# Attention on one core: a new order for VectorE's and ScalarE's instructions in the second half of each group of eight slots

## The chip, the cores and the metric

The kernel runs on one core of one Trainium2 chip. Time is that of one execution on the device, in microseconds (us). A core has five engines with queues of their own, each of which works through its instructions in the written order: TensorE (PE in the profile), VectorE (DVE), ScalarE (ACT), GpSimd (POOL) and SyncE (SP, which here issues DMAs). They meet through semaphores alone.

## The reference

Eight batches of 512 tokens with 256 features go through attention with 16 heads of 64, and then through a feed-forward network with ternary weights. In short:

```python
xn = layernorm(x)                                   # 8 x 512 x 256
q, k, v = heads(xn @ w_q), heads(xn @ w_k), heads(xn @ w_v)
sim  = (l2norm(q) * exp(scale)) @ l2norm(k).T       # per head, 512 x 512
attn = softmax(sim)
x = x + layernorm((attn @ v) @ w_out + b_out)
h = silu(lin(ln(x), w1)) * lin(ln(x), w2)
h = gelu(lin(gelu(lin(h, h1)), h2))
out = x + layernorm(lin(h, w3))
```

All of it is float32. The kernel multiplies in a rounded float32 type and keeps the accuracy by splitting an operand into a high part (the rounded value) and a low part (what the rounding left), so that most products are two or three matmuls.

## The kernel before, in words

The attention runs in 256 *slots* (`NU`), two to a head, and the program text of every engine is a loop over them. Eight slots are one *quad*, the work of four heads; `r = i % 8` is the place in the quad, and `i32_ = i % 32` the place in a batch. In slot i TensorE computes the scores of slot i (`scores`, L1047 and L1048), multiplies the probabilities of slot i - 2 with the values (`values`, L1064), and does its share of the projections for the next quad: the q and k tiles (`qk_tile`) where `tiles_of` names one, the value tiles (`v_tiles`), the turning of q and k of a pair of heads (`turn`, L1033, at r = 0 and r = 5: first k, then q), and at r = 7 the output projection of the quad before (`outp`, L1078). At i32_ = 19 and 20 it turns the next batch's normalised input (`x_turn`, L998) for the next quad's tiles.

ScalarE takes the scores out of PSUM through the exponential (`exp`, L504, writes `P`), rounds them (`p_high`, L509, writes `Ph`), evacuates a finished head every second slot (`evacuate`, L515), squares a q and k tile (`square`, L483), and writes the high parts of the turned operands (`turn_high`, L496) and of the input (`x_high`, L468). VectorE writes the low parts: of the probabilities (`p_low`, L717, writes `Pl`; slot i treats i - 1), of the turned operands (`turn_low`, L711, writes `turned`) and of the input (`x_low`, L671, writes `xl`). It also sums the squares (`head_sums`, L687), scales the tile when GpSimd has the roots (`head_scale`, L696), divides a pair of heads by their softmax sums (`normal`, L733, reads what a DMA has spread from the table `rows`), and writes the low part of that (`o_low`, L739, writes `nl`), when GpSimd has copied the high part (`o_high`, L381, writes `nh`). At i32_ = 12 and 13 GpSimd also normalises the next input and adds the last batch's result to its input (L395).

What orders this across the engines is a set of waits on counted semaphores. Those that matter here:

- `values(u)` waits for `pl` of u: TensorE at r = 7 needs the low part of the probabilities of r = 5.
- `exp(i)` waits for `pl` of i - 2.
- `outp` of a quad waits for `nl` of both its pairs. The later pair's `normal` is at r = 5 and its `o_low` at r = 6 in the loop of VectorE; both instances of `outp` stand at r = 7 in that of TensorE.
- `o_high` on GpSimd waits for `normal`, and `o_low` for `o_high`.
- The DMAs that stack the turned operands for `scores` (SP, L258 and L259) wait for all four parts of the pair; the pair turned at r = 5 is first used at the next r = 0.
- Three PSUM banks (`M.G`, called bank0 to bank2) are shared by everything but scores and values. A table computed ahead (`PLAN`) gives each user a bank and names the user before it, and `wait_bank` makes TensorE wait until that one's high and low parts are both out.

For the seven quads at whose r = 5 `i32_` is 21, the table gives the turned q of that slot the bank of the next input's first half: `PLAN["Tq", 6]` is `(0, ("x", 2))`, and so on in steps of 8 to `("Tq", 54)` behind `("x", 14)`. So TensorE's second turning at i32_ = 21 waits until `x_high(b + 1, 0)` and `x_low(b + 1, 0)` are done. The second half's bank is next used by `outp`.

Of the kernel before, what the change touches and what calls it, by code (L numbers as in the profile page):

```python
# [5 lines left out]
B, S, D, H, DH = 8, 512, 256, 16, 64  # L6
# [9 lines left out]
NP = B * HP  # L16
# [41 lines left out]
def slot(i):  # L58

    g, c = divmod(i, 2)  # L60
    return g, c, g // H, i % 8, i < NU


def tiles_of(i):

    todo = {6: [(i // 8 + 2, 0)], 0: [(i // 8 + 1, 1)], 1: [(i // 8 + 1, 2)], 2: [(i // 8 + 1, 3)]}.get(i % 8, [])
    return [NT * Q + t for Q, t in todo if Q < NQ]
# [8 lines left out]
def pair_of(i):  # L76

    n = 2 * (i // 8) + {0: 1, 5: 2}.get(i % 8, NP)
    return n if n < NP else None
# [376 lines left out]
def act_program(q, M):  # L456
# [7 lines left out]
    def x_high(b, k):  # L464
        bank = PLAN["x", 2 * b + k][0]
        q.wait_ge("xT", 2 * b + k + 1)
        q.wait_ge("v", 16 * b)
        e.activation(M.xh[:, k, :], M.G[bank][:, :], ACT.Copy).then_inc(S["xh"])  # L468
# [29 lines left out]
    def exp(i):  # L498
        q.wait_ge("s", i + 1)
        q.wait_ge("sh", 2)  # L500
        q.wait_ge("pl", i - 1)
        q.wait_ge("wl", WPOS[1])
        h = (i // 2) % H
        e.activation(M.P[:, i % 2, :], M.SB[i % 2][:, :], ACT.Exp, bias=M.sh[:, h:h + 1]).then_inc(S["exp"])  # L504
# [6 lines left out]
    def evacuate(g):  # L511
        q.wait_ge("pv", 2 * g + 2)
        q.wait_ge("on", 2 * (g // 2 - 1))
        q.wait_ge("wl", WPOS[6])
        e.activation(M.Ev[:, g % 4, :], M.OB[:, :], ACT.Copy).then_inc(S["ev"])  # L515
# [58 lines left out]
    split_w(7)  # L574
    for i in range(SLOTS):
        g, c, b, r, live = slot(i)
        if b + 1 < B and i % 32 == 21:
            x_high(b + 1, 0)
            x_high(b + 1, 1)
        if live:  # L580
            exp(i)
            p_high(i)
        if i % 2 and 0 <= i // 2 - 1 < NG:
            evacuate(i // 2 - 1)
        if i < 3:
            split_w(4 + i)
        if i in (5, 6, 12, 13):
            split_wo(i - 5 if i < 7 else i - 10)
        for u in tiles_of(i):
            square(u)  # L590
        if values_of(i) is not None:
            v_high(values_of(i))
        if pair_of(i) is not None:
            turn_high(pair_of(i), 1)
            turn_high(pair_of(i), 0)
        if HEAD <= i < HEAD + 7:
            for m in MS[i - HEAD]:
                gate(0, 0, m)
                high0(0, m)
        if copy_at(i) is not None:  # L600
            copy_piece(copy_at(i))
        if i in LOADS:
            load_piece(LOADS.index(i))
        if i == NU - 3:
            x3_high(0)
# [28 lines left out]
def vector_program(q, M):  # L634
# [32 lines left out]
    def x_low(b, k):  # L667
        bank = PLAN["x", 2 * b + k][0]
        q.wait_ge("xh", 2 * b + k + 1)
        q.wait_ge("v", 16 * b)  # L670
        e.tensor_tensor(M.xl[:, k, :], M.G[bank][:, :], M.xh[:, k, :].bitcast(f32), ALU.subtract).then_inc(S["xl"])  # L671
# [12 lines left out]
    def head_sums(u):  # L684
        q.wait_ge("sq", u + 1)
        q.wait_ge("rs", u - 1)
        e.reduce_sum(M.ss[:, u % 2, :], M.sq[:, :].rearrange("p (h d) -> p h d", d=DH), AX.X).then_inc(S["ssum"])  # L687
# [18 lines left out]
    def turn_low(n, j):  # L706
        bank = PLAN["Tk" if j else "Tq", n][0]
        q.wait_ge("thk" if j else "thq", n + 1)
        wait_stacked(q, n - 1)
        high, low = (1, 0) if j else (2, 3)  # L710
        e.tensor_tensor(M.turned[:, low, :], M.G[bank][:, :], M.turned[:, high, :].bitcast(f32), ALU.subtract  # L711
                        ).then_inc(S["tlk" if j else "tlq"])
# [14 lines left out]
    def normal(n):  # L727
        q.wait_ge("nl", n - 1)
        for odd in range(2):
            own = slice(64 * odd, 64 * odd + 64)  # L730
            q.wait_ge(f"rb{n % 2}{odd}", 16 * (n // 2 + 1))
            q.wait_ge("ev", 2 * n + odd + 1)
            e.tensor_tensor(M.on[own, n % 2, :], M.Ev[own, (2 * n + odd) % 4, :], M.Rb[own, n % 2, :],  # L733
                            ALU.mult).then_inc(S["on"])
# [147 lines left out]
    for i in range(SLOTS):  # L882
        g, c, b, r, live = slot(i)
        i32_, pb, tail, n = i % 32, i // 32 - 1, i - NU, i // 4 + 1
        early = i % 4 == 1 and i32_ != 21
        if b + 1 < B and i32_ == 21:
            x_low(b + 1, 0)
        if 0 <= i - 1 < NU:
            p_low(i - 1)
        if i < 3:  # L890
            split_w(4 + i)
        if i in (5, 6, 12, 13):
            split_wo(i - 5 if i < 7 else i - 10)
        if i % 4 == 2 and 0 <= n - 3 < NP:
            o_low(n - 3)
        if early and 0 <= n - 3 < NP:
            normal(n - 3)
        if 0 <= pb < B - 1:
            for t in {8: (0, 1), 10: (2,), 11: (3,)}.get(i32_, ()):
                finish(pb, t)  # L900
            if i32_ == 12:
                for t in range(NT):
                    out_scale(pb, t)
        if b + 1 < B:
            for t in {3: (0,), 4: (1, 2, 3)}.get(i32_, ()):
                ln1(b + 1, t)
            if i32_ == 21:
                x_low(b + 1, 1)
        for u in tiles_of(i):
            head_sums(u)  # L910
        if values_of(i) is not None:
            v_low(values_of(i))
        if pair_of(i) is not None:
            turn_low(pair_of(i), 1)
            turn_low(pair_of(i), 0)
        for u in tiles_of(i - 1) if i else []:
            head_scale(u)
        if i % 4 == 1 and not early and 0 <= n - 3 < NP:
            normal(n - 3)
        if i % 4 == 3 and 0 <= n - 2 < NP:  # L920
            invert(n - 2)
        if quad_of(i) is not None:
            add_part(quad_of(i), 0)
            add_part(quad_of(i), 1)
        if tail == 8:
            for t in range(NT):
                finish(B - 1, t)
        if tail == 9:
            for t in range(NT):
                finish2(B - 1, t)  # L930
        if HEAD <= i < HEAD + 7:
            for m in MS[i - HEAD]:
                gate(0, m)
                halves(0, 0, m)
        if i in COUNTS:
            count_piece(COUNTS.index(i))
        if i - 1 in FLAG_AT:
            flag(FLAG_AT.index(i - 1))
        if i in (NU - 9, NU - 8):
            norm3(0, 2 * (i - NU + 9))  # L940
            norm3(0, 2 * (i - NU + 9) + 1)
        if i in (NU - 6, NU - 5):
            norm3b(0, 2 * (i - NU + 6))
            norm3b(0, 2 * (i - NU + 6) + 1)
        if i == NU - 3:
            x3_low(0)
# [486 lines left out]
```

## Time and profile before

| | |
|---|---|
| time, median of 3 runs | 1764.39 us (1762.01 to 1764.74) |
| the profiled execution's own time | 1763.06 us |
| its span, first to last instruction | 1761.2 us |
| TensorE busy in the span | 1699.0 us, 96% |
| VectorE, ScalarE, GpSimd busy | 67%, 57%, 26% |
| mean granted TensorE clock | 0.992 of full speed |

The span is the profiled execution from its first to its last instruction; 1.9 us of its time lie around it. Busy times are those of instructions with work in them; an engine that waits is idle. The attention part with the changed order takes the first 1070 us or so, and the feed-forward part, which the change does not touch, the rest.

### The profile page before, as it was taken

Reading aid. Unit: us, or ns where it says so; the run is one execution under the profiler, and the core shown is the slowest. Engines: PE = TensorE matmul, PEld = TensorE weight load, DVE = VectorE, ACT = ScalarE, POOL = GpSimd, SP = SyncE. Lnnn points to the kernel's source line nnn. Section 1 sums busy time; section 2 is a strip of 40 time slices with the busy share of each in tenths; the row PEclk is TensorE's granted clock in tenths of the full one; section 3 lists DMA queues with packets and bytes.
Section 4 is the critical chain, followed back from the end, with each engine's and each line's share of the span. In section 5 each row is a group of like instructions: output and inputs, shape, how many; then the busy total and the mean of one; then the engine's idle time right before and its main releaser. Section 6 shows DMA issues by size and latency. Waiting matters only on the chain.

```text
span 1761.2 us, 24647 instructions
## 1 busy us (share of the span) xinstructions
PE 1699.0 (96%) x8584; PEld 1420.5 (81%) x8584; DVE 1181.7 (67%) x2033; ACT 1010.3 (57%) x1349; POOL 462.1 (26%) x557
## 2 busy tenths in 40 slices
PE   5999999999999999999999987999999999999998
PEld 4788888888888888888888866788888888888877
DVE  5777877877877877877877986645454545444454
ACT  4877777777877777877777775223324131423231
POOL 3423543543533534533533320000000000000000
PEclk9999999999999999999999999999999999999999
DMA  4545555555456456455455563300000000000000
GB/s 129 133 105 133 124 120 140 118 130 139 108 127 143 104 127 144 105 129 128 94 115 145 145 166 102 110 2 13 12 25 1 24 1 25 0 25 1 24 1 24
DMA packets 73473, 151.44 MB, mean 86 GB/s; under 512 B 27904, under 2 KB 28288, under 8 KB 73344
## 3 DMA queue, kind: packets, MB, share of 16 engines
q1 hardware_dynamic: 65712, 122.87, 29.8%
q10 hardware_dynamic: 6624, 23.21, 4.5%
q0 software_dynamic: 1008, 3.67, 0.5%
q8 instruction: 77, 1.26, 0.3%
q14 instruction: 52, 0.43, 0.1%
HBM read 56.91 MB, written 20.19 MB: 44 GB/s over the span
## 4 chain that ended last, share of the span: by engine, by line
PE 78%; DVE 8%; DMA 5%; issue 4%; ACT 4%; SPq 1%; POOL 1%; DVEq 0%; ACTq 0%; POOLq 0%
PE bank L1064 15%; PE pair L1142 13%; PE pair L1143 13%; PE bank L1006 12%; PE bank L1078 5%; PE pair L1047 4%; PE pair L1048 4%; PE pair L1133 3%; PE pair L1134 3%; DVE Pl L717 3%; PE bank L1033 2%; DMA rows<-Rp 2%; PE bank L1171 2%; PE bank L1172 2%; DMA work<-rows 1%
## 5 line engine op out<-in xcount | busy, mean ns | idle before, releaser
L1142 PE MATMUL pair<-hh,f 128*128 128x512 f32 x1024 | 400.7, 391 | 2.9 <-DVE hl L835 2.3
L1143 PE MATMUL pair<-hl,f 128*128 128x512 f32 x1024 | 399.4, 390 | 0.0
L1064 PE MATMUL bank<-Ph,V 128*128 128x512 f32 x1024 | 366.9, 399 | 18.5 <-DVE Pl L717 18.3
L504 ACT ACTIVATE P<-pair,sh 128x1024 f32<-128x1024 f32 x256 | 286.6, 1120 | 157.7 <-PE pair L1048 136.5
L717 DVE TENSOR_TENSOR Pl<-P,Ph 128x1024 fp32r<-128x1024 f32 x256 | 313.9, 1226 | 0.3
L552 ACT ACTIVATE hr<-pair,ct 128x512 f32<-128x512 f32 x128 | 88.3, 690 | 354.9 <-PE pair L1143 354.9
L1006 PE MATMUL bank<-w,xh 128*128 128x256 f32 (+1 forms) x1024 | 285.7, 341 | 5.4 <-DVE qk L696 2.0
L509 ACT ACTIVATE Ph<-P 128x1024 fp32r<-128x1024 f32 x256 | 271.9, 1062 | 8.1
L1064 PEld LDWEIGHTS bank<-Ph,V 128*128 128x128 f32 x1024 | 192.9, 188 | 78.2 <-issue 33.5
L1142 PEld LDWEIGHTS pair<-hh,f 128*128 128x128 f32 x1024 | 192.8, 188 | 46.6 <-DVE hl L835 6.3
L1143 PEld LDWEIGHTS pair<-hl,f 128*128 128x128 f32 x1024 | 192.8, 188 | 39.8
L373 POOL TENSOR_TENSOR rs<-ss,half 128x8 f32<-128x8 f32 x128 | 213.4, 1668 | 10.7
L1047 PE MATMUL pair<-stack 128*128 128x512 f32 x512 | 207.9, 406 | 7.2 <-issue 5.2
L1006 PEld LDWEIGHTS bank<-w,xh 128*128 128x128 f32 x1024 | 181.8, 191 | 33.2 <-DVE qk L696 2.8
L1064 PE MATMUL bank<-Pl,V 128*128 128x512 f32 x512 | 202.7, 396 | 0.0
L1048 PE MATMUL pair<-stack 128*128 128x512 f32 x512 | 201.9, 394 | 0.0
L831 DVE CAST hh<-hr 128x512 fp32r<-128x512 f32 x128 | 54.6, 427 | 215.1 <-ACT hr L552 215.0
L1006 PE MATMUL bank<-w,xl 128*128 128x256 f32 (+1 forms) x512 | 174.1, 340 | 0.0
L835 DVE TENSOR_TENSOR hl<-hr,hh 128x512 fp32r<-128x512 f32 x192 | 132.5, 690 | 15.6 <-ACT hh L559 10.5
L370 POOL TENSOR_SCALAR ss<-ss 128x8 f32<-128x8 f32 x128 | 55.3, 432 | 299.3 <-DVE ss L687 299.0
L696 DVE TENSOR_TENSOR qk<-bank,rs 128x512 f32<-128x512 f32 x128 | 87.5, 683 | 67.0 <-POOL rs L376 66.8
L687 DVE TENSOR_REDUCE ss<-sq 128x8 f32<-128x512 f32 x128 | 87.5, 684 | 60.5 <-ACT sq L483 59.2
(104 smaller groups left out, 2615.8 us busy)
## 6 DMA issues: line engine op xcount, KB each, us to landing
stack<-turned SPq DMA_DIRECT2D x128, 384.0 KB, 3.9
stack<-turned SPq DMA_DIRECT2D x128, 256.0 KB, 4.6
work<-rows SPq DMA_DIRECT2D x128, 128.0 KB, 2.9
f<-raw ACTq DMA_DIRECT2D x22, 512.0 KB, 5.1
raw<-in_h ACTq DMA_DIRECT2D x16, 512.0 KB, 3.8
xt<-in_x SPq DMA_DIRECT2D x8, 512.0 KB, 4.3
xr<-in_x SPq DMA_DIRECT2D x8, 512.0 KB, 4.6
x<-xr SPq DMA_DIRECT2D x8, 512.0 KB, 5.6
```

Of the source, the lines that this page charges most:

```text
L373: e.tensor_tensor(rs, ss, M.half[:, :], ALU.pow).then_inc(S["rs"])
L504: e.activation(M.P[:, i % 2, :], M.SB[i % 2][:, :], ACT.Exp, bias=M.sh[:, h:h + 1]).then_inc(S["exp"])
L509: e.activation(M.Ph[:, u % 3, :], M.P[:, u % 2, :], ACT.Copy).then_inc(S["ph"])
L552: e.activation(M.hr[:, u, :], M.FB[m % 4][:, :], ACT.Gelu, scale=M.sc["t1" if n == 1 else "t2"][:, m:m + 1]).then_inc(S["ea"])
L717: e.tensor_tensor(M.Pl[:, u % 3, :], M.P[:, u % 2, :], M.Ph[:, u % 3, :].bitcast(f32), ALU.subtract).then_inc(S["pl"])
L835: e.tensor_tensor(lo, raw, hi.bitcast(f32), ALU.subtract).then_inc(S["hl"])
L1006: d = e.matmul(ps, l[:, k, xs], r[:, qd, k, c0:c1], start=k == 0 and n == 0, stop=k == 1 and n == 2, skip_group_check=True)
L1047: e.matmul(ps, key, M.stack[:, k, 1, :], start=True, stop=False)
L1048: d = e.matmul(ps, key, M.stack[:, k, 2, :], start=False, stop=True)
L1064: d = e.matmul(M.OB[:, :], v, p[:, u % 3, j * 512:(j + 1) * 512], start=jt == 0 and m == 0, stop=jt == 3 and m == 2)
L1142: e.matmul(ps, w, M.hh[src][:, k, :].bitcast(to), start=k == 0, stop=False)
L1143: d = e.matmul(ps, w, M.hl[src][:, k, :].bitcast(to), start=False, stop=k == KH - 1)
```

## The change

On ScalarE, in the seven slots with i32_ = 21, the two `x_high` of the next batch's input stood ahead of the slot's `exp`; now they stand behind `exp`, `p_high` and `evacuate`. On VectorE four things move in the second half of each quad:

- `x_low(b + 1, 0)`, which stood ahead of `p_low` at i32_ = 21, stands behind it, beside `x_low(b + 1, 1)`.
- `normal` moves from r = 5 to r = 6, behind `p_low` and `turn_low`.
- `turn_low` of the pair turned at r = 5 moves to r = 6, behind `p_low(i - 1)`.
- `o_low` and the `head_sums` of the tile of r = 6 move from r = 6 to r = 7, behind the `p_low` there.

In the first half of the quad nothing moves. The number of instructions is the same. The order on TensorE, GpSimd and SP is not changed.

```diff
@@ act_program
     for i in range(SLOTS):
         g, c, b, r, live = slot(i)
-        if b + 1 < B and i % 32 == 21:
-            x_high(b + 1, 0)
-            x_high(b + 1, 1)
         if live:
             exp(i)
             p_high(i)
         if i % 2 and 0 <= i // 2 - 1 < NG:
             evacuate(i // 2 - 1)
+        if b + 1 < B and i % 32 == 21:
+            x_high(b + 1, 0)
+            x_high(b + 1, 1)
@@ vector_program
-        early = i % 4 == 1 and i32_ != 21
-        if b + 1 < B and i32_ == 21:
-            x_low(b + 1, 0)
         if 0 <= i - 1 < NU:
             p_low(i - 1)
...
-        if i % 4 == 2 and 0 <= n - 3 < NP:
+        if r in (2, 7) and 0 <= n - 3 < NP:
             o_low(n - 3)
-        if early and 0 <= n - 3 < NP:
+        if r == 1 and 0 <= n - 3 < NP:
             normal(n - 3)
...
             if i32_ == 21:
+                x_low(b + 1, 0)
                 x_low(b + 1, 1)
-        for u in tiles_of(i):
+        if r == 6:
+            if pair_of(i - 1) is not None:
+                turn_low(pair_of(i - 1), 1)
+                turn_low(pair_of(i - 1), 0)
+            if 0 <= n - 3 < NP:
+                normal(n - 3)
+        for u in tiles_of(i) if r != 6 else []:
+            head_sums(u)
+        for u in tiles_of(i - 1) if r == 7 else []:
             head_sums(u)
         if values_of(i) is not None:
             v_low(values_of(i))
-        if pair_of(i) is not None:
+        if r == 0 and pair_of(i) is not None:
             turn_low(pair_of(i), 1)
             turn_low(pair_of(i), 0)
         for u in tiles_of(i - 1) if i else []:
             head_scale(u)
-        if i % 4 == 1 and not early and 0 <= n - 3 < NP:
-            normal(n - 3)
```

ScalarE in a slot with i32_ = 21, from the value tile's high part (`V`) before it to the exponential of r = 6:

```order
 L490 ACTIVATE V<-bank 128x4x64 x2
+L504 ACTIVATE P<-pair,sh 128x1024
+L509 ACTIVATE Ph<-P 128x1024
+L515 ACTIVATE work<-bank 128x512
 L468 ACTIVATE xh<-bank 128x512 x2
-L504 ACTIVATE P<-pair,sh 128x1024
-L509 ACTIVATE Ph<-P 128x1024
-L515 ACTIVATE work<-bank 128x512
 L496 ACTIVATE turned<-bank 128x512 x2
 L504 ACTIVATE P<-pair,sh 128x1024
```

The input's high parts now have one exponential, one rounding and one evacuation in front of them that they had behind them.

VectorE in the first such quad, r = 5 to r = 7, before; here bank0 holds the first half of the input and then the turned q:

```order
L704 TENSOR_TENSOR V<-bank1,V 128x4x64 x2
L671 TENSOR_TENSOR xl<-bank0,xh 128x512
L717 TENSOR_TENSOR Pl<-P,Ph 128x1024
L671 TENSOR_TENSOR xl<-bank2,xh 128x512
L711 TENSOR_TENSOR turned<-bank1,turned 128x512
L711 TENSOR_TENSOR turned<-bank0,turned 128x512
L733 TENSOR_TENSOR work<-work 64x512 x2
L717 TENSOR_TENSOR Pl<-P,Ph 128x1024
L739 TENSOR_TENSOR nl<-work,nh 128x512
L687 TENSOR_REDUCE ss<-sq 128x8
L717 TENSOR_TENSOR Pl<-P,Ph 128x1024
```

And now:

```order
L704 TENSOR_TENSOR V<-bank1,V 128x4x64 x2
L717 TENSOR_TENSOR Pl<-P,Ph 128x1024
L671 TENSOR_TENSOR xl<-bank0,xh 128x512
L671 TENSOR_TENSOR xl<-bank2,xh 128x512
L717 TENSOR_TENSOR Pl<-P,Ph 128x1024
L711 TENSOR_TENSOR turned<-bank1,turned 128x512
L711 TENSOR_TENSOR turned<-bank0,turned 128x512
L733 TENSOR_TENSOR work<-work 64x512 x2
L717 TENSOR_TENSOR Pl<-P,Ph 128x1024
L739 TENSOR_TENSOR nl<-work,nh 128x512
L687 TENSOR_REDUCE ss<-sq 128x8
```

The second `Pl` row moves from behind the turned operands and the normals to ahead of them; the third moves from behind `nl` and the sums to ahead of them.

VectorE in the last quad of the first batch, r = 5 to r = 7, before. It is one of the 25 quads without a next input in them:

```order
L717 TENSOR_TENSOR Pl<-P,Ph 128x1024
L733 TENSOR_TENSOR work<-work 64x512 x2
L711 TENSOR_TENSOR turned<-bank2,turned 128x512
L711 TENSOR_TENSOR turned<-bank1,turned 128x512
L717 TENSOR_TENSOR Pl<-P,Ph 128x1024
L739 TENSOR_TENSOR nl<-work,nh 128x512
```

And now:

```order
L717 TENSOR_TENSOR Pl<-P,Ph 128x1024 x2
L711 TENSOR_TENSOR turned<-bank2,turned 128x512
L711 TENSOR_TENSOR turned<-bank1,turned 128x512
L733 TENSOR_TENSOR work<-work 64x512 x2
L717 TENSOR_TENSOR Pl<-P,Ph 128x1024
L739 TENSOR_TENSOR nl<-work,nh 128x512
```

`nl` has one more `Pl` in front of it than before, and the normals stand directly ahead of a `Pl`.

## Rows read from the trace of the kernel before

**Rows 1.** The page's head: busy time and share of the span by engine.
```profile
PE 1699.0 (96%) x8584; PEld 1420.5 (81%) x8584; DVE 1181.7 (67%) x2033; ACT 1010.3 (57%) x1349; POOL 462.1 (26%) x557
```

**Rows 2.** Waits of TensorE, 60 to 1120 us: us in total, times, longest.
```profile
PE bank L1064 <- DVE Pl L717: 18.3, 25, 2.2
PE bank L1078 <- DVE nl L739: 5.8, 1, 5.8
PE pair L1047 <- issue: 2.6, 3, 1.0
```

**Rows 3.** Timeline of TensorE, slots 117 to 119: start, us, what, [idle before].
```profile
513.28 0.39 PE L1048 MATMUL pair<-stack 128*128 128x512 f32 x1
...
514.90 1.03 PE L1033 MATMUL bank<-ident,qk 128*128 128x128 f32 x8
515.69 0.47 PE L1047 MATMUL pair<-stack 128*128 128x512 f32 x1
...
521.09 0.47 PE L1064 MATMUL bank<-Ph,V 128*128 128x512 f32 x1 [0.42 <-DVE Pl L717]
...
522.57 0.28 PE L1078 MATMUL bank<-oh,nh 128*128 128x256 f32 x1
```

**Rows 4.** Timeline of ScalarE, slots 117 and 118.
```profile
512.89 1.09 ACT L468 ACTIVATE xh<-bank 128x512 fp32r<-128x512 f32 x2
513.84 1.14 ACT L504 ACTIVATE P<-pair,sh 128x1024 f32<-128x1024 f32 x1
515.02 1.06 ACT L509 ACTIVATE Ph<-P 128x1024 fp32r<-128x1024 f32 x1
515.98 0.58 ACT L515 ACTIVATE work<-bank 128x512 f32<-128x512 f32 x1
516.46 1.08 ACT L496 ACTIVATE turned<-bank 128x512 fp32r<-128x512 f32 x2
```

**Rows 5.** Timeline of VectorE, slots 117 to 119.
```profile
513.71 0.68 DVE L671 TENSOR_TENSOR xl<-bank,xh 128x512 fp32r<-128x512 f32 x1
...
517.08 1.29 DVE L711 TENSOR_TENSOR turned<-bank,turned 128x512 fp32r<-128x512 f32 x2 [0.96 <-ACT turned L496]
518.29 1.40 DVE L733 TENSOR_TENSOR work<-work 64x512 f32<-64x512 f32 x2
519.72 1.23 DVE L717 TENSOR_TENSOR Pl<-P,Ph 128x1024 fp32r<-128x1024 f32 x1
521.45 0.69 DVE L739 TENSOR_TENSOR nl<-work,nh 128x512 fp32r<-128x512 f32 x1 [0.50 <-POOL nh L381]
```

**Rows 6.** GpSimd's copy of the high part: one of slot 119, then all (min/median/max).
```profile
519.75 1.66 POOL L381 CAST nh<-work 128x512 fp32r<-128x512 f32 x1 [11.69 <-DVE work L733]
...
L381 POOL CAST nh<-work x64: 611/612/1670, 77.7 to 1095.8; 128x512 fp32r<-128x512 f32 x64
```

**Rows 7.** TensorE's clock: timeline and stretches (PE, PEld, DVE, ACT, POOL, PEclk, DMA, GB/s).
```profile
67.14 0.47 PE L1047 MATMUL pair<-stack 128*128 128x512 f32 x1 [2.02 <-DMA stack<-turned]
...
68.00:70.00 2.00, 2.00 (x7) 1.51 (x6) 1.85 (x3) 1.50 (x2) 0.00 (x0) 0.51 0.88 192
70.00:72.00 2.00, 2.00 (x7) 1.60 (x6) 0.00 (x0) 0.67 (x1) 0.00 (x0) 0.64 0.23 49
...
1054.81 0.47 PE L1064 MATMUL bank<-Ph,V 128*128 128x512 f32 x1 [2.16 <-DVE Pl L717]
```

**Rows 8.** An ordinary quad, slots 101 to 103: VectorE, ScalarE, TensorE.
```profile
449.98 1.40 DVE L733 TENSOR_TENSOR work<-work 64x512 f32<-64x512 f32 x2
...
449.01 1.06 ACT L509 ACTIVATE Ph<-P 128x1024 fp32r<-128x1024 f32 x1
...
452.57 1.06 ACT L509 ACTIVATE Ph<-P 128x1024 fp32r<-128x1024 f32 x1
...
455.94 0.28 PE L1078 MATMUL bank<-oh,nh 128*128 128x256 f32 x1
```

**Rows 9.** Timeline of GpSimd, slot 77: the residual's adds.
```profile
350.45 4.28 POOL L395 TENSOR_TENSOR xr<-xr,y 128x256 f32<-128x256 f32 x4
```

## The prediction, made blind

> **What bounds the kernel now.** I began with the page's head: TensorE is busy for 96% of the span, every other engine at most 67% [rows 1]. So time is won or lost only where TensorE stands still, and the next view is its list of waits over the attention: 25 waits for `Pl` with 18.3 us in all, one for `nl`, three of 2.6 us for stacked operands that name no releaser [rows 2]. The timeline places nearly all of the first kind at r = 7, where `values` needs the low part of the probabilities of r = 5; slot 119 shows it with 0.42 us [rows 3]. On VectorE that `Pl` starts only when the normals are done, at 519.72 [rows 5], although its `Ph` (start 515.02, 1.06 us long) was out at 516.08 [rows 4]. So there are about 18 us to win here at the very most, and 3 more at the stacks. What else the moved instructions feed decides the rest: the bank of the turned q, and `nl` for the output projection, which follows `values` at r = 7 at once.
>
> **The seven quads with a next input.** I redo slot 117 (i32_ = 21) with its own durations and start-to-start distances.
>
> ScalarE. The exponential needs the scores, whose last matmul ends at 513.67 (513.28 + 0.39 [rows 3]); it now starts at 513.71 and not at 513.84. The distances stay: 1.18 to the rounding, 0.96 to the evacuation, 0.48 to the next [rows 4]. So the first `xh` starts at 516.33 and is out near 516.93 (two take 1.09, so one 0.60), and not near 513.5.
>
> VectorE. `x_low` of that half then takes 516.95 to 517.63 (0.68 [rows 5]), where before it began at 513.71.
>
> TensorE. Its second turning, of q, uses that bank. The eight transposes take 0.79 from start to start of the scores behind them [rows 3], so q's four began near 515.29. They now wait until about 517.7: TensorE, which had no gap there, stands still for 2.4 us. The scores of r = 6 start at 518.1 instead of 515.69, and slot 119 starts 2.45 later.
>
> What of that is given back before the output projection starts at 522.57? VectorE has `Pl` of r = 5 done by 519.4, so the 0.42 us stall goes, with some 0.15 (an estimate) for the slower restart behind it. The rest of the chain: turned q high 519.0, `turn_low` 519.3 to 520.6, normals to 521.9, `Pl` of r = 6 (its `Ph` is out at 521.6) to 523.1, GpSimd's copy to 523.6, `nl` to 524.3. TensorE on its side is at the output projection at 522.57 + 2.45 - 0.6 = 524.4. Both meet there: **+1.85 us in each of seven quads, +13.0**. The bounds: 1.5 if VectorE and ScalarE close up more than the rows say, 2.5 if `nl` or the second `xl` (whose tile of r = 6 needs it at about 520.6) comes later.
>
> **The clock.** A gap of 2.4 us has a second price. After the gap of 2.02 us at 67 us the granted clock of the next stretches is 0.51 and 0.64, so TensorE was at 1.2 GHz instead of 2.4 for some 3.4 us and lost 0.98 + 0.72 = 1.7 us of its time. After the gap of 2.16 us at 1054.81 I find no such stretch [rows 7]. So a gap of this size sometimes brings it. I take half of the seven: 7 x 0.5 x 1.7 = **+6**, with 0 and 11.9 as bounds.
>
> **The other quads.** In slot 101 `Pl` of r = 4 ends at 450.0 and `Ph` of r = 5 at 450.07 (449.01 + 1.06) [rows 8]. Now: `Pl` of r = 5 450.1 to 451.3, `turn_low` to 452.55, normals to 453.95 (1.40), `Pl` of r = 6 to 455.1 (its `Ph` is out at 453.63), and then `nl`. GpSimd's copy is started by the normals and so lies beside that `Pl`. Where it did so before, it took 1.66 and not 0.61 us: in slot 119 `Pl` ran 519.72 to 520.95 and the copy 519.75 to 521.41 [rows 5, 6]. That puts the copy's end at 455.6 and `nl` at 455.65 to 456.35. The output projection, which started at 455.94 [rows 8], starts at 456.4 or 456.5: +0.5 where there was no stall. Where there was a stall of 0.4, as in slot 119, it goes, and `nl` takes its place with about the same time: 0, or up to 0.5 where GpSimd's adds of the residual (4.28 us [rows 9]) stretch the `Pl` beside them.
>
> The same reading of the other 24, from slot 15 to slot 255: eight quads without a real stall +0.5 each, +4; six with the adds beside +0.4, +2.4; the last batch's two with weight counts in VectorE's queue +0.9, +1.8; four that stalled over 0.7 us in all gain 2.4; the tail +0.3. `turn_low` is 0.5 to 1 us earlier in these quads, which shortens the three stack waits by about 0.5 each [rows 2], and as much of the losses in those quads lies under what is left of them: -3. Together **+3**. The end below: all of 18.3 less the seven 0.42 and less the tail's, some -9. The end above: +0.6 in all 24, with adds, +10.
>
> In the tail, `normal` and `o_low` move behind one gate each of the feed-forward. The wait of 5.8 us for `nl` there [rows 2] is longer than the gate's instructions, so something behind both orders sets it, the DMA for the normals as far as the trace tells; I count 0.
>
> On the copy beside `Pl` the Trainium skill (SBUF — State Buffer, section "Who interferes with whom") says that a VectorE instruction with two SBUF inputs and a GpSimd one that reads SBUF exclude each other for a whole instruction, and that the one that issues first wins. By that rule the copy could also go first; then `Pl` would be 0.6 us later and `nl` at the same 456.4. So the sum is the same whichever goes first. If instead they ran side by side, as the 0.61 of the median copy would have it, `nl` would be there at 455.8 and cost nothing; that is a rival below.
>
> **Sum.** 13 + 6 + 3 = +22 us on the profiled execution's 1763.06 (span 1761.2 and 1.9 around it): 1785. The median of the runs shown is 1.3 above the profiled execution, so 1785 to 1786; I say 1785.
>
> **The rivals.**
>
> *No lower clock after the gaps.* For it: one gap of the size left the clock alone [rows 7]. Against: the other brought it. 1764.4 + 16 = 1780. Its opposite, all seven lowered: 1764.4 + 28 = 1792.
>
> *The copy is not held up by `Pl`.* Then the ordinary quads lose no 0.5 and those with stalls win theirs: -5 instead of +3, so with the clock's share 1764.4 + 13 + 6 - 5 = 1778. For it: the median copy of 0.61. Against: the one copy shown beside a `Pl` took 1.66 [rows 6].
>
> *The bank's wait is half hidden and the quads gain what they can.* If the turning waited only about 1.8 us with nothing behind `nl`, each of the seven would lose 1.3 at an unchanged clock, 9 in all, and -9 elsewhere would cancel it: 1764. This needs ScalarE to pass the exponential, the rounding and the evacuation 0.6 us faster than it does [rows 4].
>
> *The other side: faster.* Place: the same turning. If its wait were not there (if TensorE reached that turning after the low part, or `xl` did not hang on the moved `xh`), the change would take the stalls and give the stacks time: 1764.4 - 14 - 1.5 = 1749. It decides at a wait of 1.9 us: below that, with -9 in the other quads and no lower clock, the change gains. For it: 18.3 us of stalls are there [rows 2], and their `Ph` were early. Against: three distances of ScalarE's rows, all measured, put the low part 2.4 us after the turning [rows 3 to 5].
>
> **How the numbers follow.** The forecast with some of the gaps lowering the clock 0.42, none 0.25, all seven 0.10, the copy not held 0.12, cancelled 0.05, faster 0.06. The first four cases span 1778 to 1792; with the bounds of the terms (1.5 to 2.5 in each of the seven, the other quads from -9) I take 1774 to 1797. About 0.2%, 3.5 us, is what a measurement of this kernel can tell from no change. Slower by more: 0.91, which is all but the last two cases less a little for low ends together; within it: 0.04; faster: 0.05.
>
> **What the profile after would show.** TensorE's waits must have a new entry: the transposes of L1033 waiting for `xl` of VectorE (L671), seven times, 2.4 us each. If it is missing or under 1.5 us, the main term is wrong. The waits of L1064 for `Pl` should fall from 18.3 us to under 5. In their place L1078 should wait for `nl` some twenty times, 0.3 to 0.6 us each, and GpSimd's copy should take 1.66 us in nearly every second half of a quad; if the copies beside `Pl` take 0.61, that part is wrong. The granted clock over the attention should show some stretches at half speed just behind the new gaps; none, or seven, tells the clock's term. The feed-forward part from 1120 us on must be as long as before.

## The result and the profile after

The changed kernel takes 1796.84 us (median of 4 runs, 1796.09 to 1797.80) against 1764.57 (4 runs, 1762.01 to 1766.47): ratio 1.0169, 95% interval 1.0155 to 1.0184. It is 32 us slower; 21 were forecast, and the end of the range at 1797 holds it by 0.2 us. The span of the profiled execution went from 1761.2 to 1794.0 us.

The page's head of the changed kernel answers to [rows 1]:

```profile
span 1794.0 us, 24647 instructions
...
PE 1709.4 (95%) x8584; PEld 1427.1 (80%) x8584; DVE 1177.8 (66%) x2033; ACT 1012.9 (56%) x1349; POOL 453.8 (25%) x557
```

The same work, in a longer span. The waits of TensorE in the changed kernel, 60 to 1150 us (the columns of [rows 2]; lines after the changed places have moved by 4, so L1068 is the old L1064 and L1082 the old L1078):

```profile
PE bank L1082 <- DVE nl L739: 24.4, 24, 6.3
PE bank L1037 <- DVE xl L671: 15.8, 7, 2.3
PE pair L1051 <- issue: 5.3, 1, 5.3
PE bank L1068 <- DVE Pl L717: 2.4, 3, 1.1
```

The stalls for `Pl` fell from 18.3 to 2.4 us: the change does what it is for. What came in their place is larger: seven waits of the transposes for `xl`, and 24 of the output projection for `nl`, where there was one. The single wait of 5.3 us is at the start of slot 8.

The slot of the old row at 514.90 in [rows 3], slot 117, in the changed kernel; TensorE, ScalarE and VectorE:

```profile
527.23 0.60 PE L1037 MATMUL bank<-ident,qk 128*128 128x128 f32 x4
530.09 0.72 PE L1037 MATMUL bank<-ident,qk 128*128 128x128 f32 x4 [2.26 <-DVE xl L671]
530.47 0.76 PE L1051 MATMUL pair<-stack 128*128 128x512 f32 x1
531.03 0.63 PE L1052 MATMUL pair<-stack 128*128 128x512 f32 x1
...
538.16 0.28 PE L1082 MATMUL bank<-oh,nh 128*128 128x256 f32 x1
```
```profile
527.19 1.06 ACT L509 ACTIVATE Ph<-P 128x1024 fp32r<-128x1024 f32 x1
528.15 0.58 ACT L515 ACTIVATE work<-bank 128x512 f32<-128x512 f32 x1
528.63 1.07 ACT L468 ACTIVATE xh<-bank 128x512 fp32r<-128x512 f32 x2
```
```profile
529.25 1.29 DVE L671 TENSOR_TENSOR xl<-bank,xh 128x512 fp32r<-128x512 f32 x2 [2.00 <-ACT xh L468]
530.46 1.22 DVE L717 TENSOR_TENSOR Pl<-P,Ph 128x1024 fp32r<-128x1024 f32 x1
```

Read it from below: VectorE sits idle for 2.00 us until the first `xh` is out, ScalarE has put the rounding and the evacuation in front of `xh`, and TensorE stands between the turned k and the turned q for 2.26 us. Before, the eight transposes were one row without a gap. The matmuls behind the gap come every 0.43 us instead of every 0.23. Stretches of the same kernel around the gap (columns as in [rows 7]), first slot 85, then slot 117:

```profile
396.00:398.00 2.00, 0.30 (x3) 0.33 (x4) 1.14 (x2) 1.81 (x4) 0.00 (x0) 1.00 0.00 0
398.00:400.00 2.00, 2.00 (x12) 1.68 (x10) 2.00 (x4) 1.30 (x2) 0.00 (x0) 1.00 0.00 0
...
530.00:532.00 2.00, 1.91 (x8) 1.67 (x9) 2.00 (x3) 0.79 (x2) 0.00 (x0) 0.62 0.00 0
532.00:534.00 2.00, 2.00 (x7) 1.58 (x6) 1.97 (x4) 1.42 (x2) 0.00 (x0) 0.52 0.04 8
```

The gap was the same 2.26 us in both. Behind the one the clock stayed at 2.4 GHz (granted clock 1.00), behind the other it went to 1.2 GHz for over 3 us (0.62 and 0.52 over two stretches of 2 us).

An ordinary quad, slots 101 to 103 again, answers to [rows 8] and [rows 6]; VectorE, GpSimd and TensorE of the changed kernel:

```profile
461.11 2.52 DVE L717 TENSOR_TENSOR Pl<-P,Ph 128x1024 fp32r<-128x1024 f32 x2
463.56 1.28 DVE L711 TENSOR_TENSOR turned<-bank,turned 128x512 fp32r<-128x512 f32 x2
464.75 1.39 DVE L733 TENSOR_TENSOR work<-work 64x512 f32<-64x512 f32 x2
466.18 1.22 DVE L717 TENSOR_TENSOR Pl<-P,Ph 128x1024 fp32r<-128x1024 f32 x1
467.91 0.69 DVE L739 TENSOR_TENSOR nl<-work,nh 128x512 fp32r<-128x512 f32 x1 [0.51 <-POOL nh L381]
```
```profile
466.21 1.66 POOL L381 CAST nh<-work 128x512 fp32r<-128x512 f32 x1 [4.59 <-DVE work L733]
```
```profile
468.75 0.36 PE L1082 MATMUL bank<-oh,nh 128*128 128x256 f32 x1 [0.35 <-DVE nl L739]
```

GpSimd's copy lies beside `Pl` and takes 1.66 us, VectorE waits 0.51 for it, and TensorE 0.35 for `nl`.

I then took the start of each eighth slot from both timelines, counted from the span's start. The difference between the two kernels grows as follows:

| stretch | us |
|---|---|
| slots 0 to 15 | +5.8 |
| the seven quads with a next input (2.0, 2.0, 2.0, 3.2, 3.2, 2.1, 3.3) | +17.8 |
| the other quads from slot 24 to 223 | +2.9 |
| the quads of slots 224 to 247 (1.5, 1.2, 1.0) | +3.7 |
| slot 248 to the end | +2.6 |
| together | +32.8 |

The feed-forward part stayed as long as it was: from its first wait for `hl` to the end 648.6 us before and 649.4 now.

### The profile page after: what moved, and what is told of

It reads as the page before. It is cut to its first block, busy times and chain, and to the rows that moved or that the text cites. A ratio compares the mean times of both kernels' runs of the same rounds, so it can differ in the third digit from the quotient of the medians.

```text
span 1794.0 us, 24647 instructions
## 1 busy us (share of the span) xinstructions
PE 1709.4 (95%) x8584; PEld 1427.1 (80%) x8584; DVE 1177.8 (66%) x2033; ACT 1012.9 (56%) x1349; POOL 453.8 (25%) x557
## 4 chain that ended last, share of the span: by engine, by line
PE 78%; DVE 10%; ACT 4%; issue 4%; POOL 2%; DMA 2%; DVEq 0%; ACTq 0%; SPq 0%; POOLq 0%
PE bank L1068 13%; PE pair L1146 13%; PE bank L1010 12%; PE pair L1147 12%; PE bank L1082 5%; PE pair L1052 5%; PE pair L1051 5%; PE pair L1137 3%; PE pair L1138 3%; PE bank L1037 2%; POOL nh L381 2%; DVE Pl L717 2%; PE bank L1175 2%; PE bank L1176 2%; DVE work L733 2%
## 5 line engine op out<-in xcount | busy, mean ns | idle before, releaser
L1068 PE MATMUL bank<-Ph,V 128*128 128x512 f32 x1024 | 365.6, 398 | 3.0 <-DVE Pl L717 2.4
L1068 PEld LDWEIGHTS bank<-Ph,V 128*128 128x128 f32 x1024 | 194.3, 190 | 52.5 <-issue 5.8
L1051 PE MATMUL pair<-stack 128*128 128x512 f32 x512 | 210.9, 412 | 7.6 <-issue 7.6
L1052 PE MATMUL pair<-stack 128*128 128x512 f32 x512 | 205.1, 400 | 0.0
L1068 PE MATMUL bank<-Pl,V 128*128 128x512 f32 x512 | 203.2, 397 | 0.0
L381 POOL CAST nh<-work 128x512 fp32r<-128x512 f32 x64 | 65.4, 1022 | 345.0 <-DVE work L733 345.0
```

Of the source, the lines that this page charges most:

```text
L381: e.tensor_copy(M.nh[:, n % 2, :], M.on[:, n % 2, :]).then_inc(S["nh"])
L1051: e.matmul(ps, key, M.stack[:, k, 1, :], start=True, stop=False)
L1052: d = e.matmul(ps, key, M.stack[:, k, 2, :], start=False, stop=True)
L1068: d = e.matmul(M.OB[:, :], v, p[:, u % 3, j * 512:(j + 1) * 512], start=jt == 0 and m == 0, stop=jt == 3 and m == 2)
```

## The experiments

There are ten experiments, timed in three groups; all but one of their kernels start from the changed one. The kernel before, timed beside each group, had medians of 1767.11 (e1 to e4), 1766.88 (e5, e6, e7 and v1) and 1766.77 us (e8 and this one), some 2 us above the first runs. The last group has the changed kernel once more:

> The changed kernel once more, beside the kernel before on the same chip, since the kernel before was 2 to 3 us slower in the calls of the experiments than when the changed kernel was first timed. If that is the chip, the changed kernel is at 1798 to 1800 us now, the ratio stays at 1.017, and e4_first_turn gained 4 to 5 us and not 2.7. If only the kernel before scatters, it is at 1796.8 again. Theory on the clock: of its seven gaps of 2.26 us 2 to 5 are followed by a lowered clock, not the same ones as before.

Measured: 1800.40 us (1798.61 to 1802.32), ratio 1.0194 (1.0159 to 1.0229). Both kernels are 2 to 4 us slower than the first time, so each ratio is taken to the kernel before of its own group, and differences between experiments are read in the profiled executions' slot starts, which agree far better: at slot 224 the changed kernel is behind by 26.48 us in one trace and by 26.62 in the other. That they agree so well is in part luck, since three of the seven gaps lowered the clock in both, though not the same three. Behind slot 248 they don't agree: the rest costs 2.6 us more than before in the first trace and 5.9 in the second.

### The input's parts back, and the input's part alone

`e1_input_back` undoes the input's part of the change:

```diff
 # ScalarE
+        if b + 1 < B and i % 32 == 21:
+            x_high(b + 1, 0)
+            x_high(b + 1, 1)
         if live:
             exp(i)
             p_high(i)
...
-        if b + 1 < B and i % 32 == 21:
-            x_high(b + 1, 0)
-            x_high(b + 1, 1)
 # VectorE
+        if b + 1 < B and i32_ == 21:
+            x_low(b + 1, 0)
         if 0 <= i - 1 < NU:
             p_low(i - 1)
...
-                x_low(b + 1, 0)
                 x_low(b + 1, 1)
```

> The changed kernel with the next input's high and low parts back where they were (x_high ahead of the exponential of i32_ = 21, x_low of the first half ahead of p_low); VectorE's new order of Pl, turned low parts, normals and nl stays. Theory: in the changed kernel the seven quads with a next input cost 17.8 us together (four 2.0, three 3.2 with a lowered clock), by the wait of the second turning for xl. Then this kernel takes 1796.8 - 18 = 1779 us, or up to 2 us more because nl then comes late in these quads as in the others (+0.3 each), and L1037 has no wait for xl. Rival: most of that is VectorE's new order, which stays; then 1790 or more, and the seven quads are still 1.5 us or more longer than before.

Measured: 1777.97 us, ratio to before 1.0061 (1.0044 to 1.0079). The seven quads now differ from the kernel before by -0.07 to +0.02 us each; nothing waits for `xl`.

`e2_input_alone` is the kernel before with that part of the change only (the reverse of the diff above, on the old order).

> The kernel before with only the input's part of the change: x_high behind exponential, rounding and evacuation at i32_ = 21, both x_low behind p_low. VectorE's order is otherwise that of before. Theory: the turning waits 2.3 us in seven quads and 0.3 to 0.5 of it is not given back by a shorter stall for Pl, so +2.1 each and some lowered clock, 1764.5 + 18 = 1783 us (1778 to 1788). Rival: the turning's wait only shows because Pl and nl are late; alone it is hidden: 1764 to 1768.

Measured: 1784.66 us, ratio 1.0102 (1.0071 to 1.0132). Its waits of TensorE (60 to 1150 us):

```profile
PE bank L1063 <- DVE Pl L717: 17.9, 19, 3.0
PE bank L1032 <- DVE xl L671: 15.8, 7, 2.3
```

Seven waits with the same 15.8 us, beside the old stalls for `Pl`. The seven quads cost +1.7 in three cases and +3.2 or 3.3 in four. So the input's part costs about 18 us whatever VectorE's other order is (in the seven quads 17.8 us in the changed kernel and 18.1 here, by the medians 17.6 here): the rivals of both expectations fell.

### How the cost follows the place of x_high

`e5_first_half_back` puts only half 0 of the input back, on both engines. ScalarE's part is shown; on VectorE `x_low(b + 1, 0)` goes back as in e1:

```diff
 # ScalarE
+        if b + 1 < B and i % 32 == 21:
+            x_high(b + 1, 0)
         if live:
             exp(i)
             p_high(i)
         if i % 2 and 0 <= i // 2 - 1 < NG:
             evacuate(i // 2 - 1)
         if b + 1 < B and i % 32 == 21:
-            x_high(b + 1, 0)
             x_high(b + 1, 1)
```

> The changed kernel with only the first half of the next input put back (x_high of half 0 ahead of the exponential, x_low of half 0 ahead of p_low); the second half stays where the change put it. Theory: only the first half's bank is waited for, by the turning of q in the same slot, so this gives back all that e1_input_back gave: 1778 us (1776 to 1780) and no wait of the transposes for xl. Rival: any input part that ScalarE takes late costs, since the turned q's high part and the exponential of r = 6 come behind it; then the time lies near the middle, 1785 to 1790.

Measured: 1788.64 us, ratio 1.0115 (1.0087 to 1.0142). Here my theory fell. Slot 118, TensorE and VectorE (the low parts are lines 672, 718 and 712 in this kernel):

```profile
529.01 0.47 PE L1012 MATMUL bank<-w,xh 128*128 128x512 f32 x1 [1.20 <-issue]
```
```profile
526.49 0.69 DVE L672 TENSOR_TENSOR xl<-bank,xh 128x512 fp32r<-128x512 f32 x1 [1.40 <-ACT xh L468]
527.09 1.22 DVE L718 TENSOR_TENSOR Pl<-P,Ph 128x1024 fp32r<-128x1024 f32 x1
528.23 1.28 DVE L712 TENSOR_TENSOR turned<-bank,turned 128x512 fp32r<-128x512 f32 x2
```

The wait for the input's bank is gone, and behind it stood a second gate: TensorE now stands for 1.2 us in front of the q and k tile of r = 6, and the quads cost 1.3 to 1.5 each. The row names no releaser. That tile needs both halves of the new input, but the second was out at 527.18, too early for 529.01. The table of banks names another user before it, the turned k of slot 117: `PLAN["qk", 64]` is `(2, ("Tk", 30))`. Its low part is the first of the two `turned` (0.69 of 1.28 us, an estimate from the single 128x512 row above), so it is out near 528.92, and on VectorE it stands behind the `xl` that waited 1.40 us for ScalarE and a `Pl`.

`e8_second_half_behind_pl` tests that. It changes one number in e5:

```diff
-            if i32_ == 21:
+            if i32_ == 22:
                 x_low(b + 1, 1)
```

> e5_first_half_back with x_low of the second half one slot later, behind p_low of i32_ = 22, so that Pl of i32_ = 21 no longer stands behind the wait for xh. New theory on e5: the tile of r = 6 didn't wait for the second low part of the input but for the bank of the turned k, whose low part came behind that wait (528.23 + 0.69, and the tile started at 529.01). Here the turned k's low part is out 0.9 us earlier, so the wait in front of the tile falls from 1.2 to 0.2 to 0.4 us, the seven quads cost 0.4 to 0.6 us instead of 1.4, and the time is 1788.6 - 6.5 = 1782 us (1780 to 1784). Rival, the theory as it was on record for e5 and its reading: the tile waits for xl of the second half, which now comes 0.2 us later and not earlier; then the wait stays at 1.2 or more and the time at 1788 or more.

Measured: 1780.82 us, ratio 1.0083 (1.0058 to 1.0109). VectorE and TensorE of the same place:

```profile
522.53 1.23 DVE L718 TENSOR_TENSOR Pl<-P,Ph 128x1024 fp32r<-128x1024 f32 x1 [0.42 <-ACT Ph L509]
523.68 0.69 DVE L672 TENSOR_TENSOR xl<-bank,xh 128x512 fp32r<-128x512 f32 x1
524.28 1.28 DVE L712 TENSOR_TENSOR turned<-bank,turned 128x512 fp32r<-128x512 f32 x2
```
```profile
525.06 0.47 PE L1012 MATMUL bank<-w,xh 128*128 128x512 f32 x1 [0.23 <-issue]
```

The tile starts 0.78 us after the start of `turned` in both, and its wait fell to 0.23 us, the quads' cost to 0.4 to 0.5, although the second `xl` itself is later against its slot than in e5. So the gate was the turned k's bank. With e1's order, where both halves are early, it is met. The rival on record for e5 had the time right (1785 to 1790) and not the cause: ScalarE's order is the same in e8, and most of the cost went.

`e6_ahead_of_evacuation` and `e7_ahead_of_rounding` leave VectorE alone and move both `x_high` forward on ScalarE, by one and by two instructions:

```diff
 # e6, ScalarE
         if live:
             exp(i)
             p_high(i)
+        if b + 1 < B and i % 32 == 21:
+            x_high(b + 1, 0)
+            x_high(b + 1, 1)
         if i % 2 and 0 <= i // 2 - 1 < NG:
             evacuate(i // 2 - 1)
 # e7, ScalarE
         if live:
             exp(i)
+        if b + 1 < B and i % 32 == 21:
+            x_high(b + 1, 0)
+            x_high(b + 1, 1)
+        if live:
             p_high(i)
```

> The changed kernel with both x_high between p_high and evacuate at i32_ = 21, so 0.48 us earlier on ScalarE. Theory: the turning's wait follows one to one, 1.78 instead of 2.26 us; each of the seven quads costs 1.5 instead of 2.0, and a gap under 2 us lowers the clock seldom, so that most of the 3 to 4 times 1.25 go as well: 1796.8 - 3.4 - 3.8 = 1789.6 us (1788 to 1793). Rival: the length of the gap doesn't matter to the clock: 1793.4, with three to five quads still 1.2 longer than the others.

Measured: 1787.64 us, ratio 1.0119 (1.0090 to 1.0147).

> The changed kernel with both x_high between exp and p_high at i32_ = 21, so 1.44 us earlier than in the changed kernel. Theory: the wait is 0.8 us, no lowered clock, each of the seven quads costs 0.6 to 0.8 instead of 2.0 (Ph of that slot comes 1.0 later, which Pl has room for): 1796.8 - 3.8 - 9 = 1784 us (1782 to 1786), and the wait of the transposes for xl is 0.7 to 0.9 us each. Rival: the later Ph delays Pl and the values, and gives back what the turning wins: 1788 to 1792.

Measured: 1783.67 us (1779.54 to 1785.23), ratio 1.0091 (1.0063 to 1.0118). The waits of the transposes in e6, then in e7:

```profile
PE bank L1037 <- DVE xl L671: 12.4, 7, 1.8
```
```profile
PE bank L1038 <- DVE xl L672: 4.8, 7, 0.7
```

The wait follows the place of `x_high` nearly one to one: 2.26, 1.77 and 0.68 us each, so 0.49 less for a place 0.48 earlier and 1.58 less for one 1.44 earlier. With it goes the cost of a quad at full clock: 2.0, 1.5 and 0.7 us. The later `Ph` of e7 gave nothing back. And the clock: in the five profiled executions with the gap of 2.26 us (changed twice, e2, e3 and e4) 3, 3, 4, 3 and 5 of the seven quads, 18 of 35, are 1.2 to 1.6 us longer than their sisters, and not the same quads each time. With 1.77 us (e6) none of seven is, and none with 1.2 (e5) or 0.7 (e7).

### nl ahead of Pl

```diff
 # e3_nl_first, VectorE
+        if r == 7 and 0 <= n - 3 < NP:
+            o_low(n - 3)
         if 0 <= i - 1 < NU:
             p_low(i - 1)
...
-        if r in (2, 7) and 0 <= n - 3 < NP:
+        if r == 2 and 0 <= n - 3 < NP:
             o_low(n - 3)
```

> The changed kernel with o_low at r = 7 ahead of p_low and not behind it; all else as changed. Theory: what made the output projection wait is the one Pl more ahead of nl, together with GpSimd's copy being held beside it. Without it the copy lies beside nothing, takes 0.61 us if VectorE waits for it, nl is out at 1.6 to 2.2 us after the start of slot r = 7 and the output projection starts at 2.30 in all quads: -0.5 in 15 quads, -1.1 in 6, -1.5 in the last two, some -0.2 in the others, 17 us in all, 1780 us. The waits of L1082 for nl (24.4 us) fall to under 10 (the tail's 6.3 stays). Rival: nl is late because the normals themselves come one Pl later, not because of the Pl behind them; then nl moves by less than 0.6 us and the time stays above 1790.

Measured: 1778.79 us, ratio 1.0065 (1.0046 to 1.0084). A quad with the residual's adds, slot 79, GpSimd, VectorE and TensorE:

```profile
362.63 0.61 POOL L381 CAST nh<-work 128x512 fp32r<-128x512 f32 x1 [1.98 <-DVE work L733]
```
```profile
361.17 1.40 DVE L733 TENSOR_TENSOR work<-work 64x512 f32<-64x512 f32 x2
363.28 0.69 DVE L739 TENSOR_TENSOR nl<-work,nh 128x512 fp32r<-128x512 f32 x1 [0.71 <-POOL nh L381]
363.89 1.22 DVE L717 TENSOR_TENSOR Pl<-P,Ph 128x1024 fp32r<-128x1024 f32 x1
```
```profile
364.12 0.35 PE L1084 MATMUL bank<-oh,nh 128*128 128x256 f32 x1
```

VectorE waits 0.71 us for the copy, which is cheap, since `nl` is then out 2.2 us after the start of the slot. The waits for `nl` fall from 24.4 us to 9.6, of which 5.9 are the tail's. A new one of 1.4 us in six places shows at r = 0, where a q and k tile waits for the scaled tile before it, because the sums stand behind `nl` and `Pl`: slot 72 is 0.5 us longer than before. They stand there in the changed kernel too, but its TensorE comes to slot 72 later against VectorE, as it has waited for `nl` in slot 71, and that slot 72 is as long as before (4.52 us).

### The first quad

```diff
 # e4_first_turn, VectorE
             p_low(i - 1)
+        if i == 6:
+            turn_low(2, 1)
+            turn_low(2, 0)
         if i < 3:
             split_w(4 + i)
```

> The changed kernel with turn_low of the pair turned in slot 5 put ahead of the split of the output weights in slot 6 (it stands behind it in the changed kernel, and that split waits for a DMA and ScalarE). Theory: the gap of 5.3 us at the start of slot 8 comes from that; the stacked operands then leave about 2 us earlier, the gap falls to 2 to 3.5 us, and the time by 3 to 4.5 us to 1792 to 1794. Rival: the gap is the DMA's own variation, as the one of 2.0 us in the kernel before named a DMA; then 1796 to 1798.

Measured: 1794.14 us (1793.99 to 1795.64), ratio 1.0157 (1.0131 to 1.0183). Against the changed kernel that is 2.7 us less than its first time and 6.3 less than its second, neither of them timed beside it; in the traces the first two quads are 2.9 us shorter. The wait at slot 8, changed and e4:

```profile
70.85 0.76 PE L1051 MATMUL pair<-stack 128*128 128x512 f32 x1 [5.27 <-issue]
```
```profile
69.02 0.50 PE L1054 MATMUL pair<-stack 128*128 128x512 f32 x1 [3.08 <-issue]
```

And VectorE of the changed kernel ahead of it:

```profile
61.02 1.21 DVE L717 TENSOR_TENSOR Pl<-P,Ph 128x1024 fp32r<-128x1024 f32 x1
63.78 0.69 DVE L682 TENSOR_TENSOR ol<-xr,oh 128x512 fp32r<-128x512 f32 x1 [1.54 <-ACT oh L477]
64.39 1.28 DVE L711 TENSOR_TENSOR turned<-bank,turned 128x512 fp32r<-128x512 f32 x2
```

The turned low parts were moved past an instruction that exists only in slots 5, 6, 12 and 13, the split of the output weights, which waits 1.54 us for ScalarE's half of it. The gain in the trace is just below what I expected; of the 3.08 us that are left, 2.0 stood there in the kernel before, too. The rival, a DMA that varies by itself, fell: the wait is 5.27 to 5.43 us in all eight traces with the changed order there, and 3.06 and 3.08 in the two (v1 below and e4) with this one.

### All three mended

`v1_sums_and_nl_first` keeps `Pl` and the turned low parts of r = 5 ahead of the normals and takes e1's and e4's edits; at r = 7 it writes `o_low`, then `head_sums`, then `p_low` (only this part of the edit is shown):

```diff
+        if r == 7 and 0 <= n - 3 < NP:
+            o_low(n - 3)
+        for u in tiles_of(i - 1) if r == 7 else []:
+            head_sums(u)
         if 0 <= i - 1 < NU:
             p_low(i - 1)
```

> The changed kernel's idea (Pl and the turned low parts of r = 5 ahead of the normals) without its three costs: both input parts where they were before, turn_low ahead of the output weights' split in slot 6, and at r = 7 o_low and then head_sums ahead of p_low. Theory: the costs add up, and with the sums ahead of Pl the projection of r = 0 doesn't wait for head_scale: no stall for Pl or nl at r = 7 of the attention's quads, each such slot 5.2 to 5.3 us, so 1753 us (1750 to 1757), faster than the kernel before by 0.4 to 0.8%. Rival: head_sums and o_low now delay Pl of r = 6 and with it the exponential or the values of the next slots as much as they gain: 1760 to 1765.

Measured: 1751.73 us (6 runs, 1749.53 to 1753.78), ratio to before 0.9909 (0.9887 to 0.9930): 0.9% faster than the kernel before. Slot 103, VectorE and TensorE:

```profile
447.26 1.40 DVE L733 TENSOR_TENSOR work<-work 64x512 f32<-64x512 f32 x2
449.37 0.69 DVE L739 TENSOR_TENSOR nl<-work,nh 128x512 fp32r<-128x512 f32 x1 [0.71 <-POOL nh L381]
449.98 0.68 DVE L687 TENSOR_REDUCE ss<-sq 128x8 f32<-128x512 f32 x1
450.57 1.22 DVE L717 TENSOR_TENSOR Pl<-P,Ph 128x1024 fp32r<-128x1024 f32 x1
```
```profile
450.73 0.28 PE L1088 MATMUL bank<-oh,nh 128*128 128x256 f32 x1
```

The projection starts with no wait. At slot 248 this kernel is 14.7 us ahead of the kernel before, of which the seven quads give 4.6 (0.6 to 0.7 each, where the stall for `Pl` was). No q and k tile waits for the scaled tile at r = 0 any more, as expected with the sums ahead of `Pl`.

## Why the prediction was right, and where it was short

*What bounds the kernel, and what the change removes.* Right. The stalls for `Pl` fell to 2.4 us, under the 5 named, and v1 shows that they were worth some 14 us.

*The seven quads.* Right in mechanism, place and size. The forecast gap was 2.4 us, measured 2.26; the forecast cost without the clock 1.85 each, 13 in all, measured 2.0 to 2.1 where the clock stayed, so 14.1. e1, e2, e6 and e7 show it from four sides. What the step didn't see, since nothing in its sum hung on it, is the second gate that e5 and e8 showed behind the first: the turned k's bank.

*The clock.* Half of the gaps were to lower it; 3 of 7 did here and 18 of 35 over five executions. The price per case was 1.2 to 1.6 us, not 1.7. It was 1.2 to 1.3 in the changed kernel, where the slot of r = 7 is 5.45 to 5.49 us long at full clock and 5.17 to 5.18 behind a lowered one, as `nl` is then there in time; in e2 and e3, where that slot is 5.17 or 5.18 either way, it was 1.5 to 1.6. The two rivals at either end fell. In sum, the step of 13 + 6 = 19 stands against 17.8 measured: the closeness owes something to two errors of opposite sign, 1.1 too little for the gaps and 2.3 too much for the clock. That half of the gaps would do it was drawn from one case of two, and its fit is luck.

*The ordinary quads.* Right in mechanism. The forecast start of the projection, 2.8 us after the slot's start, is the measured 2.82 (468.75 less 465.93), and the copy beside `Pl` took 1.66 us. The rival of a copy that isn't held fell: those beside a `Pl` took 1.66, and the ones without 0.61 (in e1, 28 copies of 1.66 or 1.67 beside a `Pl` and 36 of 0.61 beside none). The Trainium skill's rule, that such a pair excludes each other for a whole instruction (SBUF — State Buffer, "Who interferes with whom"), agrees with these rows as far as they go: `Pl` keeps its 1.22 us, and the copy, which starts 0.03 us after it, ends 0.47 us after its end, a little sooner than a whole copy of 0.61 would. Of the 24 waits for `nl`, 13 are of 0.3 to 0.4 us, as the sign named them; the six with the residual's adds are of 0.9, where at most 0.5 was named. From slot 24 to 223 the quads that lost did so by 6.4 us together, as forecast (4 + 2.4); those that gained did so by 3.5 and not by the 5.4 of the forecast (2.4 + 3). So this stretch cost 2.9 us where its terms come to +1.

*Where it was short.* By 11 us, nearly all of it in that last term or left out of it. The term was +3, and what it stood for measured 15: 2 us more in the stretch just named, and three other places. The seven quads took 1.2 less than the forecast.

The first two quads cost 5.8 us where I had counted none: I read the order of a quad from one in the middle and did not look at what stands only in the first, the splits of the output weights that the turned low parts now come behind. Of the 5.8, 3.7 are there at the start of slot 8, where the wait is 3.25 us longer than before. The other 2.1 are in slots 8 to 15. About 1.0 of them is the first output projection, in slot 15, which waits 2.01 us where `values` waited 1.01 before; its row names no releaser, but `nl` ends at 104.17:

```profile
103.48 0.69 DVE L739 TENSOR_TENSOR nl<-work,nh 128x512 fp32r<-128x512 f32 x1 [0.50 <-POOL nh L381]
```
```profile
104.38 0.36 PE L1082 MATMUL bank<-oh,nh 128*128 128x256 f32 x1 [2.01 <-issue]
```

About 1.1 is the clock: behind the wait at slot 8 TensorE worked at 1.2 GHz for 5.7 us, and for 3.4 in the kernel before (granted clock 0.50 from 70.85 to 74.25 us and 0.67 from there to 77.65). e4, which has 3.4 us as well, loses 1.0 in slots 8 to 15; e3 and v1, which write `nl` first, have a wait of 0.9 us in slot 15.

The last three quads cost 3.7 and not 1.8, since the weight counts in VectorE's queue lengthen the way to `nl` there: 1.22 us for a count ahead of `Pl`, and waits for `nl` of 1.37, 1.58 and 2.37 us (e3 took that back).

The tail after slot 248 cost 2.6 us where I said 0.3. Of that a part is the wait for `nl` of 2.89 us in slot 255, which took the place of one for `Pl` of 2.12. How much the change costs here stays open: the 5.9 us of the second trace come from the same program. There the gaps of 2.15 and 2.88 us in slots 250 and 255 were followed by 1.2 GHz; in the first trace those places had gaps of 1.09 and 2.89 us, and neither was.

*The range and the chances.* That 1797 holds the result by 0.2 us is luck: the second time the same kernel took 1800.4, with the kernel before 2 us slower as well. The range was also narrower than its stated bounds, which with 17.5, 11.9 and 10 would reach 1804, and 0.6 in each of 24 quads is 14.4 and not 10. The chance of 0.91 for a slower kernel is more than the 0.89 that its four cases add up to.

*The other side.* The rival of a faster kernel gave as its condition that the turning doesn't wait for the moved input. e1 meets that condition and is still 0.6% slower than before; the sign turned only in v1, which writes `nl` and the sums ahead of `Pl` and mends the first quad as well. So that rival was wrong in its own terms: the -9 to -14 us that it took from the stalls could not be had with this order.

## What to carry to other kernels

When an instruction is moved behind others on its engine, list everyone who waits for its result, a buffer's next user included, and not only the one that the move is for. Here 25 stalls, most of them of 0.4 us, were mended by an order that opened seven waits of 2.3 us and 23 of 0.8 on average. A wait also hides those behind it: as long as the first gate opens last, a trace doesn't show the second, and mending the first uncovers it, as in e5. An order is right only when the second and third waits in the row are met too. And read the first and the last repetition of a loop by themselves, since what is only there stands in the same queue.

## What the runs showed of the hardware

A gap on TensorE of 2.26 us, always the same, was followed by a stretch at 1.2 GHz in 18 of 35 cases, and gaps of 1.77, 1.2 and 0.7 us at the same place or one slot on in none of 21. That half a microsecond of gap separates one case in two from none here I had not expected.

The other gaps that the twelve traces show between 60 and 1110 us, and that began at full clock, were followed by 1.2 GHz as follows. These gaps differ in place and in what went before them, and the one of 1.89 us, in slot 248 of e4, shows that a gap under 2 us can do it; so the counts give odds for this kernel and no bound.

| gap, us | followed by 1.2 GHz |
|---|---|
| 1.89 and 1.95 | 1 of 2 |
| 2.00 to 2.01 (slot 15 of eight kernels) | 0 of 8 |
| 2.02 to 2.18 | 4 of 11 |
| 2.31 to 2.41 | 7 of 10 |
| 2.87 to 2.95 | 6 of 9 |
| 3.06 and more | 16 of 16 |

The other figure is the copy beside `Pl`: GpSimd's rounding copy of 128x512 took 1.66 or 1.67 us whenever a `Pl` of VectorE started just ahead of it, and 0.61 or 0.62 in all other cases.
